# Attention stage of a transformer block: where a pair of heads issues its loads, and what stands in the queue ahead of a row of maxima

## The reference, cut to what matters

```python
x = x + layernorm(attn(layernorm(x)))
x = x + layernorm(moe(layernorm(x)))

# attn, per batch and head
scores = einsum('nhbqd,nhbkd->nhbqk', qb, kb) / sqrt(d)    # query block x its key window
ctx    = einsum('nhbqk,nhbkd->nhbqd', softmax(scores), vb)
qg     = take_along_axis(q, idx)                           # 64 chosen queries
g_ctx  = softmax(einsum(qg, k) / sqrt(d)) @ v
ctx    = ctx.at[bn, bh, idx].set(g_ctx)
```

## Time and profile before

| | us |
|---|---|
| median of 3 runs | 886.73 |
| lowest and highest run | 881.71, 887.17 |
| profiled execution | 884.11 |
| its span, first to last instruction | 882.4 |
| TensorE busy in the span | 810.5 (92%) |
| VectorE, ScalarE, GpSimd busy | 570.1, 406.9, 144.0 |

### The profile page before, as it was taken

One profiled execution on the slowest core, in us unless ns is written; L12 is line 12 of the kernel. 1 busy time (PEld: TensorE's weight loads), 2 busy tenths in 40 slices (PEclk: granted clock), 3 DMA queues, 4 the chain that ended last, 5 costly groups with the idle time before them and its releaser, 6 DMA issues.

```text
span 882.4 us, 13837 instructions
## 1 busy us (share of the span) xinstructions
PE 810.5 (92%) x5076; PEld 660.8 (75%) x5076; DVE 570.1 (65%) x1215; ACT 406.9 (46%) x801; POOL 144.0 (16%) x228
## 2 busy tenths in 40 slices
PE   2999999998899998899699999799999999999994
PEld 1676868676777777677487777699999999887883
DVE  5644997367888656575368654356666667748565
ACT  2433242325565666566544334356666666623120
POOL 4100000220110212222124631200000000012222
PEclk9999999999999999999699989899999999999998
DMA  6687545875777667661228742447787677545444
GB/s 203 190 298 229 182 133 170 254 227 141 211 199 202 170 182 199 192 180 54 74 96 290 241 160 100 133 148 210 228 250 225 218 219 211 180 155 181 153 132 143
DMA packets 117444, 162.39 MB, mean 184 GB/s; under 512 B 17316, under 2 KB 65188, under 8 KB 117376
## 3 DMA queue, kind: packets, MB, share of 16 engines
q1 hardware_dynamic: 113792, 153.54, 57.2%
q0 software_dynamic: 3584, 7.97, 3.1%
HBM read 107.24 MB, written 55.05 MB: 184 GB/s over the span
## 4 chain that ended last, share of the span: by engine, by line
PE 64%; DVE 17%; DMA 7%; issue 4%; ACT 4%; POOL 2%; SPq 1%; DVEq 0%; POOLq 0%; ACTq 0%
PE bank L163 41%; PE wide L163 18%; PE wide L167 3%; DVE MX L160 3%; PE bank L167 2%; DVE SG L160 2%; DMA H<-scr_oe,FG 2%; DMA QSe<-MR 2%; DMA scr_v<-vt 1%; DVE STC L279 1%; DVE CX L1398 1%; DVE XT L149 1%; DMA WQH<-MR 1%; DVE W13L L149 1%; DVE SIL L149 1%
## 5 line engine op out<-in xcount | busy, mean ns | idle before, releaser
L163 PE MATMUL bank<-XT,W13H 128*128 128x256 f32 (+1 forms) x1056 | 244.1, 326 | 3.4 <-DVE XT L149 3.4
L163 PEld LDWEIGHTS bank<-XT,W13H 128*128 128x128 f32 x1056 | 176.9, 192 | 19.8 <-DVE XT L149 2.2
L163 PE MATMUL bank<-XT,W13L 128*128 128x256 f32 (+1 forms) x528 | 170.6, 323 | 0.0
L163 PE MATMUL wide<-W2H,HH 128*128 128x512 f32 x352 | 118.8, 404 | 4.0 <-DVE CX L1398 3.8
L163 PEld LDWEIGHTS bank<-XT,W13L 128*128 128x128 f32 x528 | 101.2, 192 | 8.3
L160 DVE TENSOR_REDUCE MX<-wide 128x1 f32<-128x192 f32 (+1 forms) x128 | 77.7, 648 | 28.4 <-PE wide L163 23.4
L157 ACT ACTIVATE PT<-bank 128x512 f32<-128x512 f32 x128 | 73.2, 594 | 31.2 <-PE bank L163 27.2
L149 DVE TENSOR_TENSOR SIL<-bank,SIL 128x256 f32<-128x256 f32 (+1 forms) x72 | 36.9, 512 | 74.5 <-ACT SIL L157 73.9
L157 ACT ACTIVATE SIL<-bank 128x256 f32<-128x256 f32 (+1 forms) x72 | 32.7, 454 | 110.6 <-PE bank L163 109.7
L163 PEld LDWEIGHTS wide<-W2H,HH 128*128 128x128 f32 x352 | 68.3, 194 | 20.3 <-DVE CX L1398 5.5
L163 PE MATMUL wide<-W2L,HH 128*128 128x512 f32 x192 | 76.9, 401 | 0.0
(11 more groups left out here) (206 smaller groups left out, 1471.6 us busy)
## 6 DMA issues: line engine op xcount, KB each, us to landing
R<-in_L_ffn_W_dram SPq DMA_DIRECT2D x48, 512.0 KB, 5.0
scr_q<-hl SPq DMA_DIRECT2D x16, 512.0 KB, 4.2
scr_k<-hl SPq DMA_DIRECT2D x16, 512.0 KB, 3.8
R<-in_L_ffn_sw_dram SPq DMA_DIRECT2D x12, 512.0 KB, 5.0
QSe<-scr_q SPq DMA_DIRECT2D x36, 128.0 KB
KSe<-scr_k SPq DMA_DIRECT2D x36, 128.0 KB, 2.9
scr_v<-vt SPq DMA_DIRECT2D x16, 272.0 KB, 2.4
R<-_attn_hidden_states_dram SPq DMA_DIRECT2D x16, 256.0 KB, 3.9
```

The costliest lines, as they stand in the source:

```text
L163: return do("pe", lambda g: g.matmul(ps, a, b, start=start, stop=stop, skip_group_check=True), after, mark=mark)
```

## The change: the order in which a pair issues its loads

`load_head` is taken apart into `load_queries` and `load_keys`. The queries stay in steps 1 and 5, and the keys come one step later, in steps 2 and 6. The value loads move from step 2, ahead of the row of step 4, to step 4, behind it. The weights move from step 7, ahead of the row of the next step 0, to step 0, behind that row, and are spread over more pairs: each group of `load_13` in two halves over pairs 2 to 7, and the groups of `load_2` in pairs 8, 9 and 10 (before: `load_13` in pairs 2 to 4, `load_2` in pairs 5 to 7). The number of transfers and their bytes stay the same.

```diff
-        def load_13(j, g):
+        def load_13(j, g, only=(0, 1)):
...
-            dma("sp", s13[g], lambda e: e.dma_start(rb[:, :, c0:c1], v1[:, :, c0:c1]), after)
+            if 0 in only:
+                dma("sp", s13[g], lambda e: e.dma_start(rb[:, :, c0:c1], v1[:, :, c0:c1]), after)
+            if 1 not in only:
+                return
+            busy13[g] = []
...
-        def load_head(n, after=()):
+        def load_queries(n, after=()):
...
+            heads[n] = dict(qi=qi, q=qb, mq=mq)
+
+        def load_keys(n, after=()):
...
-            heads[n] = dict(qi=qi, q=qb, ki=ki, k=kb, mq=mq, mk=mk)
+            heads[n].update(ki=ki, k=kb, mk=mk)
+
+        def load_head(n, after=()):
+            load_queries(n, after)
+            load_keys(n, after)
...
                     if k in (1, 5) and i < 14:
-                        load_head(2 * i + 4 + k // 5)
-                    if k == 2 and i % 2 == 0 and i < 14:
-                        load_v(i // 2 + 1)
-                    if k == 7 and 2 <= i < 8:
-                        (load_13 if i < 5 else load_2)(0, (i - 2) % 3)
+                        load_queries(2 * i + 4 + k // 5)
+                    if k in (2, 6) and i < 14:
+                        load_keys(2 * i + 4 + k // 6)
...
                 if k == 0 and 0 < i < 16:
                     row_shift(2 * i + 1, ST_)
+                    if 2 <= i < 8:
+                        load_13(0, (i - 2) // 2, (i % 2,))
+                    elif 8 <= i < 11:
+                        load_2(0, i - 8)
...
                 if k == 4 and i < 15:
                     row_shift(2 * i + 2, ST_)
+                    if i % 2 == 0 and i < 14:
+                        load_v(i // 2 + 1)
```

More of the change, by code:

```diff
@@ L296, in sandwich @@
         m13, m2 = {}, {}
-        def load_13(j, g):
+        def load_13(j, g, only=(0, 1)):
             v1, v3 = [a.rearrange("(k p) n -> p k n", p=P) for a in jobs[j][0:2]]
-            after, busy13[g] = busy13[g], []
+            after = busy13[g]
             c0, c1 = 256 * g, min(256 * g + 256, H)
-            dma("sp", s13[g], lambda e: e.dma_start(rb[:, :, c0:c1], v1[:, :, c0:c1]), after)
+            if 0 in only:
[3 more added lines that the diff above has]
+            busy13[g] = []
             if g == 2:
@@ L361, in load_head @@
             qi, qb, qfree = QS.take()
-            ki, kb, kfree = KS.take()
             for part, l in enumerate((0, 1, 1)):
@@ L365, in load_head @@
                     f(qb[32 * part:32 * part + 32, :]), qd[l, rows, toks]), qfree + list(after))
+            heads[n] = dict(qi=qi, q=qb, mq=mq)
+        def load_keys(n, after=()):
+            b, h = divmod(n, HEADS)
+            toks = slice(b * SEQ, (b + 1) * SEQ)
+            rows = slice(h * HD, (h + 1) * HD)
+            ki, kb, kfree = KS.take()
             for part, l in enumerate((0, 1, 0)):
```

## The result

The changed kernel takes 878.82 us (median of 20 runs, 875.25 to 882.77), the kernel before 882.60 us in its 20 runs. The ratio is 0.995, with an interval from 0.9931 to 0.997: 0.3 to 0.7% faster, or about 4.4 us. The profiled execution took 875.69 us with a span of 873.9 us.

The account below looks back on a forecast made before the run. TensorE, busy 810.5 of 882.4 us, bounds the kernel; only late rows in the attention stage can be won. 3.0 + 1.5 + 0.6 - 0.5 = 4.6 us, giving 879.5 or 882.1 by base; forecast halfway, 880.8, range 876.5 to 887.5.

Parts of the forecast that it names:

- second rival: Pairs 10 and 11: later weights delay row 23's chain, idle before head 22 grows, clock falls; 883.5 us; chance 0.21.
- Row 2: Pair 0: with the values behind it, the row goes out 1.4 us earlier and nothing stalls; gain 3.0 us.
- clock term: Pair 1: the slow clock after the idle time before head 2 goes; 0.95 us, or 1.7 by the skill's page.
- Row 7: Pair 3: with the weights behind it, the row lands in time; gain 1.5 us, bounds 0 and 1.5.
- Row 18: Pair 8: with the values behind it, the row's idle time goes; gain 0.6 us, between 0.4 and 0.7.
- Pairs 10 and 11: Row 22 gains 0.3 us, but weights delay the context's store and row 23; together a loss of 0.5 us.
- row 23 still late: Sign of being right in the profile: TensorE still idles before head 23, 2.03 us in the kernel before.
- The halving: Even pairs: only the context's store comes between queries and keys; taken at nothing, between +0.4 and -0.4 us.
- The first rival: Seven odd rows come late behind 1.3 MB of values and heads; 19 us at worst, time 890.6 us; chance 0.07.
- the landing of 4.9 us: Time an odd row has to land after its issue; rows landed in 2.8 to 3.7 us, one in 7.64.

Follow-up runs that it names:

- v0_only: Kernel before with one move: the values loaded in pair 0 go behind row 2; ratio to the kernel before 0.996.
- w_only: Kernel before with only the weights moved behind the odd row and spread over pairs 2 to 10; ratio to the kernel before 1.0019.
- late_w2: Changed kernel with the last 512 KB of weights in pair 12 instead of pair 10; ratio to the kernel before 0.9962.
- x1_behind: late_w2 with the store that waits for GpSimd's addition put behind the next odd row; ratio to the kernel before 0.9905.
- vw_whole_heads: Changed kernel without the halving: values and weights moved, heads loaded whole in steps 1 and 5; ratio to the kernel before 1.0006.
- h_only: Kernel before with only the heads' loads halved, queries in steps 1 and 5, keys in 2 and 6; ratio to the kernel before 1.0064.
- v_only: Kernel before with only the value loads moved behind the even row; ratio to the kernel before 1.0063.
- w13_even: Changed kernel with the three 1 MB weight groups whole in pairs 2, 4 and 6, behind even row and values; ratio to the kernel before 1.0066.
- best2: w_whole with the GpSimd-waiting store behind the odd row and the next stage's first two tiles in step 0 of pair 9; ratio to the kernel before 0.9905.
- w_whole: Changed kernel with whole weight groups in pairs 2 to 7, behind the odd row; ratio to the kernel before 0.9943.
- best3: best2 with head 3 loaded behind row 1 at the start of the stage; ratio to the kernel before 0.989.

## Why the prediction was right, point by point

**The sum.** Forecast 4.6 us, measured 4.0 in the stage of one profiled execution and 4.4 by the ratio. The forecast of 880.8 us was taken from a base halfway between two, 885.4; the median is 878.8, mostly because the 20 runs of before have a median of 882.6, 2.8 us below that base. Of the 4.0 us, 0.36 come from pair 6, for which I had no term and which varies by itself (below); so the terms that I named gave 3.6, and the nearness of the sum is in part luck. (In the second rival 885.4 - 2.1 is 883.3, not 883.5; nothing hangs on it.)

**Row 2.** Forecast 3.0 us, measured 2.28 in pair 0 and 0.90 in pair 1, 3.2 in all, with the clock at 1.00 in pair 1. v0_only shows that this one move is worth 3.5 us by itself (0.4 to 6.6 by its interval). The rows of the changed kernel show that the row was issued at once, with the values behind it:

```profile
199.79 0.25 ACT L145 ACTIVATE MR<-bank 8x128 fp32r<-8x128 f32 x1
...
200.06 0.64 SPq L435 DMA_DIRECT2D WQH<-MR  x1
200.75 0.52 SPq L392 DMA_DIRECT2D late<-scr_v  x1
```

The clock term was 0.90 to 0.95 us by the pair's length. The Trainium skill, TensorE: Matmul & The Clock Gate, section Terms, gave 1.7 by its formula; the trace bears out the smaller figure here.

**Row 7.** Forecast 1.5 us, measured 1.37. I forecast that the row would go out 0.8 us later than before relative to row 6 (5.4 us behind it) and would land in time. It went out at 234.37, 5.7 us behind row 6 at 228.68, and nothing waited. w_only, with the weights alone moved, shows the same 14.24 us for pair 3. But v0_only had 14.24 us in pair 3 with the weights still ahead of the row, so this term is not always there to win.

**Row 18.** Forecast 0.6, measured 0.68.

**Pairs 10 and 11.** Forecast a loss of 0.5 us within -2.0 and +0.5, measured 1.64. The term was too small. I took row 22 as a gain of 0.3, but it was issued as soon as it was made and TensorE could use it only 5.9 us later, at 346.02. The matmul's line names the keys of head 24 as what ended that wait, which this product doesn't need; the weight load of the same product names the row.

```profile
331.97 0.63 SPq L435 DMA_DIRECT2D WQH<-MR  x1
...
333.12 1.18 SPq L322 DMA_DIRECT2D R<-in_L_ffn_sw_dram  x2
...
340.13 0.69 SPq L435 DMA_DIRECT2D late<-MR  x1
...
346.02 0.50 PEld L163 LDWEIGHTS bank<-late 97*128 97x128 f32 x2 [3.13 <-DMA late<-MR]
...
349.55 0.34 SPq L790 DMA_DIRECT2D scr_x<-XX  x1
...
352.74 0.68 SPq L435 DMA_DIRECT2D late<-MR  x1
```

The rate was a small part of the error: I counted 261 GB/s from one microsecond, and the stretch from 332 to 348 us ran at 237 GB/s with its engines full; for 512 KB that is 0.2 us. Half of the second rival's mechanism came true in this trace: idle time of 2.94 us before head 22 and a slow clock behind it. The other half, idle time before head 23, did not, and my own sign of being right, "row 23 still late", failed in the same way. Row 23 is issued 4.2 us after it was made, and TensorE doesn't wait for it since it arrives later itself. late_w2 and x1_behind then show both causes, one behind the other: first the weights, then the store that waits for GpSimd.

**The halving.** Taken at nothing, and that was wrong as a step. Alone it costs 0.6%, and together with the moved values it seems to gain (vw_whole_heads 1.0006 against 0.995). My sentence that SyncE's list runs on until something waits was right. I named the one thing that does wait there, the context's store, but priced it at 0.4 us for one key load, and didn't follow it to what all of it means: keys, store and values in one crowd ahead of the even row, up to 3.04 us of idle time in h_only. In the changed kernel the values are out of that crowd, so the total came out near in spite of the wrong step; its effect there lies in pairs 10 and 11, in a term that was off by 1.1 us.

**The first rival.** With 1.3 MB ahead, the odd rows didn't wait. v_only and w13_even, with 2.3 MB, show the mechanism in full, with waits up to 3.45 us (v_only's 4.94 is the store's). No run tested the landing of 4.9 us from which it was to begin; the 1.01 us with 1.8 MB in v_only are the nearest. The estimate by the Trainium skill, DMA: Bandwidth & Descriptors, section Anatomy of one DMA, had an odd row late by 0.2 us with 1.34 MB; the changed kernel's trace shows no such wait. That section gives its formula for DMAs issued by GpSimd, which I passed over; these are issued by SyncE.

**What stays open.** The three single moves give +0.6, +0.2 and +0.6%, all three together -0.5%. The sum of parts is no guide here. I can show for each run which row waits, but not derive the 2.0% between the sum of the singles, +1.5%, and the whole. And pair 6 took 14.2 to 14.8 us in nine traces and 15.2 to 17.9 in five (best2, late_w2, w_whole, w13_even, x1_behind), with TensorE idle mostly for nothing that the profile names:

```profile
289.50 0.33 PE L167 MATMUL bank<-ident,PG 128*128 128x128 f32 x1 [1.30 <-issue]
```

That is x1_behind; ScalarE had like gaps there, and the clock is at 0.50 to 0.66 from 291 to 295. From this pair on GpSimd gathers the chosen queries of the second batch, but best3 has this too and took 14.25. I didn't test it.

## What to carry to other kernels

A small transfer on the critical chain pays twice for what stands ahead of it in its list: for the issue of each transfer (0.3 to 0.7 us here, up to 2.59 in the earlier trace rows, where the DMA engines were full), and for their bytes in the DMA engines. Put it first and let the bulk follow, but then look at the next small transfer and at the bytes between the two: 1.3 MB did no harm here, 2.3 MB did in four places of five. An instruction that waits for another engine divides the list; what is moved behind it comes late and in a crowd, so first find the waits, and keep stores that wait for a slow engine behind the urgent row. And when a line names an engine that had long been done, look at the weight load beside it before you believe that no row is late.

## What the runs showed of the hardware

A row of 4 KB that landed within 2.8 us in a quiet queue took 5.7 us in w_only and almost 6 in the changed kernel, issued without delay in both. Its size tells nothing of its time.

After idle times of 2.01 and 2.03 us TensorE's granted clock fell to the 1.2 GHz level, after 1.90 us in the same trace it did not. But the length of an idle time doesn't tell whether the clock falls: in w_only it fell after 1.90 us before head 2, in h_only after 1.12 us before head 6 and in v0_only after 0.87 us before head 22, while in v_only it stayed at 1.00 after 2.31 us before head 7. The rows are of w_only, h_only and v_only, in this order, with columns as in the earlier trace rows; the clock is the third number from the end.

```profile
204.28 0.50 PE L163 MATMUL bank<-WQH,WKH 97*128 97x256 f32 x2 [1.90 <-DMA WQH<-MR]
205.00:206.00 1.00, 1.00 (x8) 0.40 (x8) 1.00 (x2) 0.68 (x2) 0.00 (x0) 0.50 0.81 213
...
236.00:237.00 1.00, 1.00 (x7) 0.40 (x8) 0.98 (x2) 0.45 (x2) 0.00 (x0) 0.50 0.74 144
...
243.61 0.50 PE L163 MATMUL bank<-QSe,KSe 97*128 97x256 f32 x2 [2.31 <-DMA QSe<-MR]
244.00:245.00 1.00, 1.00 (x11) 0.58 (x12) 0.00 (x0) 0.64 (x2) 0.00 (x0) 1.00 0.97 229
```

Nor does it tell how long the clock stays low. With 2.94 us the changed kernel shows 0.50 from 346 to 352 us; vw_whole_heads, with 2.96 us before head 23, shows it from 357 to 360. The first microsecond of the changed kernel's stretch:

```profile
346.00:347.00 1.00, 0.98 (x3) 0.74 (x4) 0.00 (x0) 0.14 (x1) 0.92 (x1) 0.50 1.10 249
```
